# Pre-activation convolutions on one core: from band matrices over rows to channels on partitions, with 32x32 array tiles

## What is computed

```python
def _conv(inputs, u, v, w, b):
    kern = jnp.einsum('lj,lk,li->ijkl', u, w, v)
    out = lax.conv_general_dilated(inputs, kern, window_strides=(1, 1), padding='SAME',
                                   dimension_numbers=('NHWC', 'HWIO', 'NHWC'))
    return jax.nn.relu(out + b)

def _gn(v, G=8, eps=1e-5):
    g = v.reshape(B_, H_, W_, G, C_ // G)
    m = jnp.mean(g, axis=(1, 2, 4), keepdims=True)
    s = jnp.var(g, axis=(1, 2, 4), keepdims=True)
    return ((g - m) / jnp.sqrt(s + eps)).reshape(v.shape)

x = x + _conv(_gn(x), L0_u, L0_v, L0_w, L0_b)
x = x + _conv(_gn(x), L1_u, L1_v, L1_w, L1_b)
```

## Time and profile before

| | us |
|---|---|
| median of three runs | 5744.07 (5743.53 to 5744.48) |
| the profiled execution | 5745.21 |
| its span in the trace | 5743.4 |
| PE busy | 5165.1 |
| DVE busy | 4424.2 |
| ACT busy | 3427.1 |

### The profile page before, as it was taken

How to read it: one execution, slowest core, us unless ns; L and a number is a source line. 1 busy time by engine, 2 the same in 40 slices (tenths; PEclk the granted TensorE clock), 3 DMA queues, 4 the chain that set the end, 5 groups by cost and what they waited for, 6 DMA issues and landing times.

```text
span 5743.4 us, 82893 instructions
## 1 busy us (share of the span) xinstructions
PE 5165.1 (90%) x30976; PEld 3930.7 (68%) x30976; DVE 4424.2 (77%) x7315; ACT 3427.1 (60%) x5377; POOL 26.0 (0%) x25
## 2 busy tenths in 40 slices
PE   6999999999999999999999999999999999999997
PEld 5766676667666766676667666766677666766675
DVE  6777777777777777777777777777777777777776
ACT  4656665566556655665566556655665566556654
POOL 1000000000000000000000000000000000000000
PEclk9999999999999999999999999999999999999999
DMA  3211222122222112221122212222212222212211
GB/s 123 118 63 75 107 120 120 71 82 91 120 120 91 78 74 120 120 102 80 62 120 120 120 62 87 95 120 120 84 71 89 120 120 91 90 62 120 120 61 61
DMA packets 61156, 555.35 MB, mean 97 GB/s; under 512 B 11105, under 2 KB 28001, under 8 KB 28001
## 3 DMA queue, kind: packets, MB, share of 16 engines
q10 hardware_dynamic: 33728, 520.10, 21.9%
q1 hardware_dynamic: 27040, 29.95, 1.7%
HBM read 268.99 MB, written 268.44 MB: 94 GB/s over the span
## 4 chain that ended last, share of the span: by engine, by line
PE 53%; DVE 44%; issue 1%; DMA 1%; ACT 0%; SPq 0%; DVEq 0%; ACTq 0%
DVE image L434 34%; PE ps_b L320 31%; PE ps_z L285 15%; DVE z L423 10%; PE ps_t L271 6%; PE ps_b L314 1%; DMA relu<-seam_r 1%; SPq L244 0%; PE ps_s L329 0%; ACT transposed L355 0%; DMA image<-in_x 0%; ACT relu L398 0%; DVE bn L445 0%; DVE band L210 0%; DVE relu L207 0%
## 5 line engine op out<-in xcount | busy, mean ns | idle before, releaser
L285 PE MATMUL ps_z<-mix,transposed 128*128 128x160 f32 (+2 forms) x17408 | 2566.4, 291 | 488.1 <-DVE z L423 460.1
L285 PEld LDWEIGHTS ps_z<-mix,transposed 128*128 128x128 f32 x17408 | 2317.5, 191 | 636.6 <-ACT transposed L355 349.8
L355 ACT ACTIVATE transposed<-ps_t,norm 128x512 f32<-128x512 f32 (+1 forms) x2304 | 1722.1, 755 | 1075.3 <-PE ps_t L271 1070.5
L434 DVE TENSOR_TENSOR image<-image,relu 128x512 f32<-128x512 f32 x2048 | 2061.1, 1071 | 18.6 <-DMA relu<-seam_r 18.3
L320 PE MATMUL ps_b<-z,band 128*128 128x512 f32 x4096 | 1851.2, 601 | 10.3 <-DVE z L423 0.7
L398 ACT ACTIVATE relu<-ps_b,parameters 128x512 f32<-128x512 f32 x2048 | 1408.4, 688 | 498.8 <-PE ps_b L320 471.4
L423 DVE COPY z<-ps_z 128x480 f32<-128x480 f32 (+1 forms) x1536 | 1031.6, 672 | 779.0 <-PE ps_z L285 778.9
L271 PE MATMUL ps_t<-shift,image 128*128 128x128 f32 x8704 | 1330.1, 273 | 37.0 <-DVE small L217 19.7
L320 PEld LDWEIGHTS ps_b<-z,band 128*128 128x128 f32 x4096 | 748.0, 190 | 858.5 <-issue 819.8
L445 DVE BATCH_NORM_STATS2 bn<-image 128x6 f32<-128x512 f32 x2048 | 1263.6, 715 | 17.3 <-DMA image<-in_x 17.3
L271 PEld LDWEIGHTS ps_t<-shift,image 128*128 128x128 f32 x8704 | 1026.9, 142 | 115.8 <-issue 96.0
(11 more groups left out here) (38 smaller groups left out, 246.7 us busy)
## 6 DMA issues: line engine op xcount, KB each, us to landing
out<-image ACTq DMA_DIRECT2D x64, 4096.0 KB, 11.3
image<-in_x ACTq DMA_DIRECT2D x60, 4096.0 KB, 13.4
image<-in_x SPq DMA_DIRECT2D x4, 4096.0 KB, 27.6
seam_z<-z SPq DMA_DIRECT2D x256, 32.0 KB
relu<-seam_r SPq DMA_DIRECT2D x512, 8.0 KB, 1.9
shift<-in_shifts SPq DMA_DIRECT2D x1, 192.0 KB, 2.4
z<-in_seams SPq DMA_DIRECT2D x1, 192.0 KB, 2.6
parameters<-in_params SPq DMA_DIRECT2D x2, 66.0 KB, 2.1
```

Of the source, the lines that this page charges most:

```text
L285: last = nc.tensor.matmul(ps_z[i % PS_Z][:, (a - lo) * C:(z + 1 - lo) * C], T[:, i % T_SLOTS, n * P:(n + 1) * P], mix[layer_of(k)][:, a - ...
L355: nc.scalar.activation(T[:, i % T_SLOTS, 0:n], ps_t[i % PS_T][:, 0:n], ACT.Identity, scale=norm[:, k % 2, 0:1], bias=norm[:, k % 2, 1:2]). ...
L434: nc.vector.tensor_tensor(x_ch, x_ch, R[:, :, s, w0:w0 + ADD_PX], ALU.add).then_inc(added, 1)
```

## The change

It is a new program for the same result; nothing of the old loops is left.

**Layout.** 32 partitions (a quad) hold two neighbouring pixels' 16 channels; the four quads hold four stretches of 64 pixels of the width. The free dimension is the image height (256). Loads bring an image to `raw` with 32 image rows on each quad. DVE turns 32x32 blocks of it (`turn_in`, L459, eight instructions of 128 x 1024 an image) into `evens`. The first conv reads `evens` and gives `odds`, which is displaced by one pixel, and the second reads `odds` and gives `result`. DVE turns it back (`turn_out`, L478, eight an image) into `pixels`, which ACT's queue stores.

**Convs.** A conv of an image has 8 rounds. A round is 96 matmuls for the conv (6 taps x 16 array tiles, L265 or L295) and 32 that carry the input to the output's place for the residual (L276 or L302). Each uses 32 rows and 32 columns of the array and 256 columns of data. The inner loop goes over the four column tiles of one row tile, so four matmuls in a row share their rows of the array and differ in the columns; the four row tiles write to four different banks. The norm's scale is multiplied into the weights (`scale_weights`), its mean is taken care of by padding (`pad_evens`, `pad_odds`) and a bias (`biases`).

**Behind a round.** ACT applies relu to 128 x 1024 numbers of PSUM (L345, L348), then DVE adds the residual half of PSUM (`evacuate`, L469). There are two sets of four banks. Every conv round, every sum of partial statistics (`group_sums`) and every bias product takes the next set in the order of `uses`, and waits until the one before last is read out.

**Statistics.** ACT squares with an accumulator (L335, L355), POOL adds the eight slots (`fold`, L208, seven adds an image), DVE reduces.

**Order.** Image p goes through eight rounds of its first conv, then eight rounds of image p-1's second conv, in which the statistics of odds p and evens p+1 are closed.

The program has 131,072 matmuls for the convs and the residual (64 images x 16 rounds x 128), besides 2,624 small ones. The core of the diff:

```diff
-def on_scalar(i):
-    return i % 3 == 2
...
+IN_DMAS, OUT_DMAS, HALO0_DMAS, HALO1_DMAS = QUADS, QUADS, 2, 3
+FOLDS = SLOTS - 1
+EVENS_IN_A = {5: (1,), 6: (2,), 7: (3,)}
+EVENS_IN_B = {0: (4,), 1: (5,), 2: (6,), 3: (7, 8)}
+ODDS_SUM, ODDS_SCALE, ODDS_PAD = 1, 2, 3
+EVENS_REDUCE, EVENS_SUM, EVENS_SCALE, BIAS = 4, 5, 6, 7
...
+    take("sum", 0, 0)
+    take("bias", -1)
+    for p in range(IMAGES + 1):
+        if p < IMAGES:
+            for e in range(ROUNDS):
+                take("conv", 0, p, e)
+        for e in range(ROUNDS):
+            if p:
+                take("conv", 1, p - 1, e)
+            if e == ODDS_SUM and p < IMAGES:
+                take("sum", 1, p)
+            if e == EVENS_SUM and p + 1 < IMAGES:
+                take("sum", 0, p + 1)
+            if e == BIAS and p < IMAGES:
+                take("bias", p)
+    return table
...
+        raw = sb("raw", [P, HB, RUN])
+        N0 = sb("evens", [P, QUADS * SLOTS + 1, HP])
+        T1 = [sb(f"odds{i}", [P, QUADS, SLOTS + 1, HP]) for i in range(2)]
+        T2 = [sb(f"result{i}", [P, QUADS, H]) for i in range(T2_SLOTS)]
...
+        ps = [ctx.enter_context(nc.psum_tensor(f"ps{i}", [P, QUADS, BANK], fp32)) for i in range(SETS)]
...
+            return ps[USE[key] % SETS]
...
+            def load(p):
+                if p:
+                    sp.wait_ge(turned_in, SLOTS * p)
+                for r in range(QUADS):
+                    sp.dma_start(raw[Q * r:Q * (r + 1), :, :], x_quads[p, r]).then_inc(image_in, 16)
+            def halo_of_evens(p):
...
+            def halo_of_odds(p):
+                sp.wait_ge(evac0, ROUNDS * p + 1)
...
+            for p in range(IMAGES):
+                halo_of_odds(p)
+                if p + 1 < IMAGES:
+                    halo_of_evens(p + 1)
+                if p + 2 < IMAGES:
+                    load(p + 2)
...
+            for p in range(IMAGES):
+                for d in range(2, SLOTS + 1):
+                    pool.wait_ge(turned_in, SLOTS * p + d)
+                    if d == 2:
+                        if p:
+                            pool.wait_ge(reduced0, p)
+                    else:
+                        pool.wait_ge(folded, FOLDS * p + d - 2)
+                    nc.gpsimd.tensor_tensor(fold[:], chunk(1) if d == 2 else fold[:], chunk(d),
+                                            ALU.add).then_inc(folded, 1)
...
-            def transposes(t, k, i):
...
-            def rows_step(t, k, i):
...
+            def take(*key):
+                if USE[key] < SETS:
+                    return
+                kind, *of = ORDER[USE[key] - SETS]
+                if kind == "conv":
+                    y, p, e = of
+                    pe.wait_ge(evac1 if y else evac0, ROUNDS * p + e + 1)
...
+            def group_sums(y, p):
+                take("sum", y, p)
+                pe.wait_ge(reduced1 if y else reduced0, p + 1)
+                to = psum("sum", y, p)
+                for q in range(QUADS):
+                    for r in range(QUADS):
+                        done = nc.tensor.matmul(to[Q * q:Q * (q + 1), r, 0:2], same_group[Q * r:Q * (r + 1), :],
+                                                sums[y][Q * r:Q * (r + 1), :], start=True, stop=True)
+                done.then_inc(filled, 1)
...
+            def conv0(p, e):
+                take("conv", 0, p, e)
+                if e == 0:
+                    pe.wait_ge(scaled0, p + 1)
+                    pe.wait_ge(padded0, p + 1)
+                    pe.wait_ge(halo0, 16 * HALO0_DMAS * (p + 1))
+                to = psum("conv", 0, p, e)
+                for t in range(NTAP):
+                    side, i = t // TAPS, t % TAPS
+                    for r in range(QUADS):
+                        for q in range(QUADS):
+                            at = t if e or q or r else NTAP + 2 + t
+                            nc.tensor.matmul(to[Q * q:Q * (q + 1), r, 0:H],
+                                             w0[Q * r:Q * (r + 1), at * Q:(at + 1) * Q],
+                                             N0[Q * r:Q * (r + 1), SLOTS * q + e + side, i:i + H],
+                                             start=(t == 0), stop=False, skip_group_check=True)
...
+                for side in range(SIDES):
+                    for r in range(QUADS):
+                        for q in range(QUADS):
+                            done = nc.tensor.matmul(to[Q * q:Q * (q + 1), r, H:2 * H],
+                                                    perm[Q * r:Q * (r + 1), side, :],
+                                                    N0[Q * r:Q * (r + 1), SLOTS * q + e + side, 1:1 + H],
+                                                    start=False, stop=(side == 1), skip_group_check=True)
+                done.then_inc(filled, 1)
...
+            def stats_of_evens(p, d):
+                act.wait_ge(turned_in, SLOTS * p + d)
+                if SLOTS * p + d > 1:
+                    act.wait_ge(stats0, SLOTS * p + d - 1)
+                nc.scalar.activation(junk[0][:], N0[:, d::SLOTS, 1:1 + H], ACT.Square,
+                                     accum_out=acc[0][:, d - 1:d]).then_inc(stats0, 1)
+            def relu(y, p, e):
+                key = ("conv", y, p, e)
+                if e == 0:
+                    act.wait_ge(biased, p + 2 if y else p + 1)
+                act.wait_ge(filled, USE[key] + 1)
+                to, got = R[CONV[key] % R_SLOTS][:], psum(*key)[:, :, 0:H]
+                if y == 0:
+                    ins = nc.scalar.activation(to, got, ACT.Relu, bias=bias[:, 0:1],
+                                               accum_out=acc_relu[:, e:e + 1])
+                else:
+                    ins = nc.scalar.activation(to, got, ACT.Relu, bias=bias[:, 1:2])
...
+            def pad_odds(p):
+                act.wait_ge(scaled1, p + 1)
+                act.wait_ge(halo1, 16 * HALO1_DMAS * (p + 1))
...
+            for p in range(IMAGES + 1):
+                if p < IMAGES:
+                    for e in range(ROUNDS):
+                        relu(0, p, e)
+                        if e:
+                            stats_of_odds(p, e - 1)
+                        if e == 1 and p >= 2:
+                            store(p - 2)
+                        if p + 1 < IMAGES:
+                            for d in EVENS_IN_A.get(e, ()):
+                                stats_of_evens(p + 1, d)
+                for e in range(ROUNDS):
+                    if p:
+                        relu(1, p - 1, e)
+                    if e == 0 and p < IMAGES:
+                        stats_of_odds(p, ROUNDS - 1)
+                    if p == IMAGES and e == 1:
+                        store(p - 2)
+                    if p + 1 < IMAGES:
+                        for d in EVENS_IN_B.get(e, ()):
+                            stats_of_evens(p + 1, d)
+                    if p < IMAGES:
+                        if e == ODDS_SUM:
+                            root(1, p)
+                        if e == ODDS_PAD:
+                            pad_odds(p)
+                        if p + 1 < IMAGES:
+                            if e == EVENS_SUM:
+                                root(0, p + 1)
+                            if e == EVENS_SCALE:
+                                pad_evens(p + 1)
...
+            def turn_in(p, d):
+                dve.wait_ge(image_in, 16 * IN_DMAS * (p + 1))
+                if p:
+                    dve.wait_ge(filled, USE["conv", 0, p - 1, min(d, ROUNDS - 1)] + 1)
+                pixels_in = raw[:].rearrange("p j (q k x) -> p q j k x", q=QUADS, x=Q)[:, :, :, d - 1, :]
+                nc.vector.transpose(N0[:, d::SLOTS, 1:1 + H].rearrange("p q (j h) -> p q j h", h=Q),
+                                    pixels_in).then_inc(turned_in, 1)
+            def evacuate(y, p, e):
+                key = ("conv", y, p, e)
+                n = ROUNDS * p + e
+                dve.wait_ge(relued, CONV[key] + 1)
+                if y and n >= T2_SLOTS:
+                    dve.wait_ge(turned_out, n - T2_SLOTS + 1)
+                to = T2[n % T2_SLOTS][:] if y else T1[p % 2][:, :, e, 1:1 + H]
+                nc.vector.tensor_tensor(to, psum(*key)[:, :, H:2 * H], R[CONV[key] % R_SLOTS][:],
+                                        ALU.add).then_inc(evac1 if y else evac0, 1)
+            def turn_out(p, e):
+                n = ROUNDS * p + e
+                dve.wait_ge(evac1, n + 1)
+                if e == 0 and p:
+                    dve.wait_ge(image_out, 16 * OUT_DMAS * p)
+                to = pixels[:].rearrange("p j (q k x) -> p q j k x", q=QUADS, x=Q)[:, :, :, e, :]
+                nc.vector.transpose(to, T2[n % T2_SLOTS][:].rearrange("p q (j h) -> p q j h", h=Q)
+                                    ).then_inc(turned_out, 1)
...
+            def reduce_partials(y, p):
+                if y == 0:
+                    dve.wait_ge(folded, FOLDS * (p + 1))
+                    dve.wait_ge(stats0, SLOTS * (p + 1))
```

(68 more changed lines are left out.)

663 lines of the change are left out of this document (268 added, 395 removed).

## The result

The changed kernel takes **9470.27 us** (median of four runs, 9463.22 to 9474.34) where the kernel before took 5744.27 beside it: 1.649 times as long, interval 1.646 to 1.651. The forecast was 4610, the range 4300 to 7950. Its profiled run has a span of 9465.3 us at a mean granted clock of 0.856.

The account below looks back on a forecast made before the run. PE's matmul streams were taken as the bound: 55.5 us an image plus 14.2 of waits, 4461 for 64 images, 4521 with first image, tail and 1.8 around the span, plus 90 for the clock: 4610 us; range 4300 to 7950.

Parts of the forecast that it names:

- Can PE be fed?: PE's instruction supply: 2,090 packets at 1.1 us, 2.2 ms beside the work; a record pair needed every 0.0136 us.
- Full overlap, 3.47 us a round: Conv rounds on PE: all 16 tiles stream at once, so 128 matmuls take 3.47 us, an image 55.5 us.
- the seam: Two tiled matmuls in the old kernel's trace, the only tiles there; read as two column tiles overlapping fully, 12 ns a pair.
- Rival 1 (start rate): PE starts no more than one record in 28 ns over a long run: 7920 us, chance 0.12.
- the 28 ns of the sums: In the old trace, the sums' two records, with next to no stream, start 0.028 us apart; rival 1's start rate.
- Rival 2: On PE, matmul halves run in order (28.4 ms), or only four column tiles of a row tile overlap (14.7 ms); chance 0.10.
- Rival 3: DVE's adds wait on POOL, up to 2.3 us more each in the first conv: 5060 us; chance within a shared 0.19.
- rival 4: A term at its upper bound: transposes 4630, adds 4920, ACT 4800, both clock falls 4880 us; chance within a shared 0.19.
- The other engines: Per image ACT 44 us, DVE 45 us, POOL 16.5 us, all under PE's 55.5.
- PE's waits for data: Places where PE waits for relus, adds, sums, scaled weights: 13.7 us an image, 14.2 with small products.
- The clock: PE falls to 1.2 GHz after waits; half a fall an image, 90 us, between 0 and 360.

Follow-up runs that it names:

- e7: Changed kernel with each round's six tap passes as a PE loop using the first tap, and next to no image traffic: 6127.3 us, 1.065 times the kernel before.
- m1: Test of PE alone, no image traffic: six written-out stages of 32x32-tile matmuls and two loops; the loop of 16 tiles, 256 columns took 0.63 us a pass.
- m2: Test of PE alone, every stage a loop, with fewer tiles or columns; 16 tiles 0.63 us a pass, 12 tiles 0.56, 128 columns 0.51, 64 columns 0.48.

## Why the prediction was wrong, step by step

- **"Can PE be fed?" failed.** It set a packet's transfer time, 1.1 us, against the span: 2.2 ms beside the work. The transfer was right (1.0 us measured). But the step took a latency for the whole price. One packet is on its way at a time, so what counts is the distance from one to the next, 3.8 us: 7.9 ms for 2,090, and 9.4 with the waits behind images. The kernel before couldn't show it by a wait, with 260 packets in 5743 us, one in 22. A lower bound was nowhere in its rows, and I took the absence of a price for no price. The Trainium skill (Runtime: NRT & Kernel Launch, Instruction fetch mechanics) has the same packets of 256 instructions and calls the cost of crossing from one to the next mostly hidden; here it isn't, 28% of the chain is that.
- **"Full overlap, 3.47 us a round" failed too,** by itself enough for the sign. From two column tiles of the seam it went to sixteen. Eight overlap fully; sixteen take 0.63 us a pass, a round 5.01 (e7), and the kernel 6127 us. I had written that it turns slower from 19.5 ns a pair; it takes 19.7 in m1's loop and 19.6 in e7's rounds. Why sixteen tiles lose what eight don't stays open. The 12 ns a pair of the seam was a short burst: the forecast's 13.6 lies below the 15 that no stage of a loop got under.
- **Rival 1 (start rate)** had the right sign and a wrong cause: the 28 ns of the sums isn't a start rate, since pairs start 15 ns apart for long. Its 7920 us rested on 28 ns, and that packets without traffic give 8020 is chance. The range's upper end rested on it as well, and no term had the images' traffic in it: 1.45 ms.
- **Rival 2** was right to be small: with halves in order or with four tiles at once no pass of 16 tiles could take 0.63 us. **Rival 3** didn't happen: adds of the first conv take 1226 ns, those of the second 1225. Of **rival 4** no bound was reached but the clock's: it fell 4.8 times an image, for two.
- **The other engines** came out near: DVE's adds 1.23 us for 1.24, transposes 1.23 for 1.23, relu 1.12 for 1.14, squares with their accumulators 1.05 + 0.19 for 1.38, POOL's adds 2.19 for 2.36. An image takes 42.8 us on DVE and 37.5 on ACT, for 45 and 44.
- **PE's waits for data**, 13.7 us an image (14.2 with the small products), are best read in e7, where a round 5.01 long hides more than one of 3.47: PE waits there for DVE some 7 us an image (442 us in all, and 58 more, most of it at the start). So the 13.7 were not tested as they stand.
- **The clock** was to cost 90 us, by half a fall an image. It fell 308 times and was at 0.50 for 2.73 of the 9.47 ms. Packets hid most of that: those of their distances under 6 us that lie wholly at 0.50 are 4.03 us on average, those at 1.00 3.75, and a line through all of them gives an estimated 130 us. In e7, where packets don't hide it, the clock was at 0.50 for 754 us; matmuls started every 31.5 ns there and every 19.9 at 1.00, an estimated 240 us. So the term was too small, and 130 lies near 90 by luck.

## What to carry to other kernels

Count PE's instructions as well as its streams: divide the time by its instruction packets, and where less than some 4 us is left for one of 256 instructions, the supply sets the time, and packets that wait behind large transfers come on top. The absence of a wait in a kernel that doesn't load a resource says nothing of its rate; measure it alone before splitting work into small tiles. Here small tiles came to pay, by 4.4%, with longer streams (512 columns an instruction) and paced transfers of 256 KB together.

## What was not expected of the hardware

- A packet of 256 instructions lands every 3.3 us at best and 3.8 on average; with image loads and stores of 1 MB, three distances an image are over 9.
- Eight 32 x 32 tiles overlap fully (0.86 us a pass at clock 0.50), twelve and sixteen don't (0.56 and 0.63 at 1.00 for streams of 0.43); no stage took less than 15 to 16 ns a pair of load and matmul, at 0.50 or 1.00.
- PE can be busy all the time and be granted 1.2 GHz (clock 0.50): so in m2's stages of 1 x 4 and 2 x 4 tiles, and in its loop of 16 tiles with 64 columns from 33 us on; the stages 4 x 1, 4 x 2 and 3 x 4 with 256 columns had 1.00 in the stretches shown. With short streams the whole kernel ran at 0.532.
